# Gated attention on one NeuronCore: six gate tiles moved from VectorE quotients to ScalarE, and one order of products and idle matmuls for all passes

## What is computed

```python
scale = HEAD_DIM ** 0.5
scores = jnp.einsum('bhqd,bhkd->bhqk', q, k) / scale
scores = jax.nn.sigmoid(scores - mu) * jnp.exp(scores)
scores = scores / jnp.sum(scores, axis=-1, keepdims=True)
out = jnp.einsum('bhqk,bhkd->bhqd', scores, v)
```

## Time and profile before

| | us |
|---|---|
| median of three executions | 1508.39 |
| lowest, highest | 1506.9, 1511.1 |
| the profiled execution | 1511.61 |
| its span in the profile | 1509.7 |
| granted TensorE clock, mean | 0.948 of full |
| TensorE matmuls busy | 1274.5 (84%) |
| VectorE busy | 1133.8 (75%) |
| ScalarE busy | 1120.9 (74%) |
| POOL busy | 349.2 (23%) |

### The profile page before, as it was taken

The page is one execution under the profiler, slowest core; times in us unless marked ns, Lnnn a source line. Parts: engine busy times, 40 slices in busy tenths (PEclk is TensorE's granted clock), DMA queues, the critical chain, the costliest instruction groups (busy, mean ns, idle before and its releaser), DMA issues.

```text
span 1509.7 us, 22834 instructions
## 1 busy us (share of the span) xinstructions
PE 1274.5 (84%) x8290; PEld 657.9 (44%) x8290; DVE 1133.8 (75%) x2049; ACT 1120.9 (74%) x1604; POOL 349.2 (23%) x434
## 2 busy tenths in 40 slices
PE   6599999885888888888888887788999988888996
PEld 3244444462111111122111245566777866666774
DVE  8888886366697887976779656768756676776898
ACT  4177788747999999999999633455476576877985
POOL 2500001541000000002000034545555557431000
PEclk9599999996899999999999997999999999999998
DMA  5300100004000000100000120013333243011111
GB/s 191 111 24 25 44 24 4 2 5 150 0 22 18 4 22 1 37 21 1 21 1 0 57 92 1 1 31 96 94 112 91 78 112 140 21 36 29 43 50 56
DMA packets 41088, 70.50 MB, mean 47 GB/s; under 512 B 6416, under 2 KB 14864, under 8 KB 40208
## 3 DMA queue, kind: packets, MB, share of 16 engines
q1 hardware_dynamic: 40976, 69.05, 15.0%
HBM read 59.26 MB, written 9.76 MB: 46 GB/s over the span
## 4 chain that ended last, share of the span: by engine, by line
PE 32%; DVE 26%; ACT 20%; issue 13%; POOL 6%; DMA 2%; SPq 1%; POOLq 0%; ACTq 0%; DVEq 0%
ACT SHARED L1144 12%; DVE SHARED L1180 8%; PE PS L823 5%; PE PS L787 3%; PE PS L645 2%; DVE PS L2255 2%; PE PS L712 2%; PE PS L2045 2%; PE PS L2047 2%; PE PS L2046 2%; PE PS L1359 2%; DVE X L284 1%; POOL SHARED L2078 1%; PE PS L2054 1%; DVE STX L266 1%
## 5 line engine op out<-in xcount | busy, mean ns | idle before, releaser
L1144 ACT ACTIVATE SHARED<-PS 128x1536 f32<-128x1536 f32 (+1 forms) x346 | 457.5, 1449 | 14.8 <-PE PS L1036 9.8
L1180 DVE TENSOR_TENSOR SHARED<-SHARED 128x1536 f32<-128x1536 f32 (+1 forms) x170 | 276.6, 1700 | 34.7 <-ACT SHARED L1144 34.7
L1036 PE MATMUL PS<-QS,KS 48*128 48x512 bf16 (+1 forms) x1006 | 208.2, 397 | 83.0 <-ACT SHARED L1144 76.5
L803 ACT ACTIVATE SHARED<-PS 128x512 f32<-128x512 f32 (+3 forms) x384 | 163.6, 493 | 72.1 <-PE PS L791 63.6
L1036 PEld LDWEIGHTS PS<-QS,KS 48*128 48x128 bf16 (+1 forms) x1006 | 38.3, 94 | 297.8 <-ACT SHARED L1144 271.1
L2045 PE MATMUL PS<-ROUNDED 128*128 128x512 f32 x328 | 138.0, 421 | 15.7 <-DVE ROUNDED L2242 7.8
L1049 PE MATMUL PS<-SHARED,Vg 128*16 128x512 f32 x1024 | 139.5, 619 | 7.2 <-DVE SHARED L1180 6.9
L732 DVE TENSOR_REDUCE NM<-PS 128x2 f32<-128x1024 f32 (+3 forms) x128 | 124.0, 1018 | 13.2 <-PE PS L718 12.6
L2047 PE MATMUL PS<-ROUNDED 128*128 128x512 f32 x328 | 130.7, 398 | 0.0
L2046 PE MATMUL PS<-ROUNDED 128*128 128x512 f32 x328 | 130.5, 398 | 0.0
L2175 ACT ACTIVATE ROUNDED<-PS 128x512 fp32r<-128x512 f32 x100 | 59.8, 598 | 91.8 <-DVE PS L2255 91.8
(11 more groups left out here) (279 smaller groups left out, 2483.6 us busy)
## 6 DMA issues: line engine op xcount, KB each, us to landing
SHARED<-wx SPq DMA_DIRECT2D x64, 256.0 KB, 3.2
SHARED<-in_moe SPq DMA_DIRECT2D x3, 1600.0 KB, 10.8
SHARED<-wx SPq DMA_DIRECT2D x16, 224.0 KB, 2.9
SHARED<-kx SPq DMA_DIRECT2D x32, 96.0 KB
KS<-kx SPq DMA_DIRECT2D x32, 96.0 KB
SHARED<-wx SPq DMA_DIRECT2D x16, 192.0 KB, 2.8
SHARED<-wx SPq DMA_DIRECT2D x16, 160.0 KB, 2.8
qx<-SHARED SPq DMA_DIRECT2D x16, 128.0 KB, 2.4
```

Of the source, the lines that this page charges most:

```text
L803: act.activation(PB[t % 3][:, h, q0:CH], bank(RING0[n % 3], q0), ACT.Exp, scale=SCORE_SCALE)\
L1036: ins = pe.matmul(bank((v % 2) * GRP + f - a), KS[g % 2][r, h // 2, kt * P:kt * P + P], QS[g % 2][r, h // 2, qh * CH:(qh + 1) * CH], start ...
L1144: act.activation(dst, PS[:, (v % 2) * GRP * CH:((v % 2) * GRP + b - a) * CH], ACT.Exp if second == qh else ACT.Sigmoid, scale=SCORE_SCALE)\
L1180: dve.tensor_tensor(ex_tile(j), ex_tile(j), GR[w % RING][:, 0:(b - a) * CH], ALU.mult)\
```

## The change

`QUOTIENT`, `WEIGHT_LATE` and the two functions of the quotient are taken out. All 16 passes have 11 gate tiles, scored by TensorE (3 more matmuls in each of the six passes), activated by ScalarE (1 more tile in each) and multiplied by VectorE. All follow `WEIGHT_AT` and `FILL_AT`. ScalarE's activation for exp(mu) and its wait ahead of the stage are gone.

```diff
-        WEIGHT_LATE = (6, 7, 9, 11, 13, 15, 17, 19)
...
-        QUOTIENT = (0, 2, 4, 6, 8, 14)
-        QS1 = [arena(24064, CH), arena(31744, CH), arena(31744 + CH, CH)]
-        EMU = MU1[:, 3:4]
-
-        def by_quotient(n, j):
-
-            return n % 2 == 1 and n // 2 in QUOTIENT and j == 0
-
-        SCORED = [(n, j) for n in range(4 * NG) for j in range(NTILE) if not by_quotient(n, j)]
+        SCORED = [(n, j) for n in range(4 * NG) for j in range(NTILE)]
...
         def pe_tile(pe, n, j):
...
-            if by_quotient(n, j):
-                return
...
-                            if (WEIGHT_LATE if hf in QUOTIENT else WEIGHT_AT)[kt] == at:
+                            if WEIGHT_AT[kt] == at:
                                 pe_weighted1(pe, hf, kt)
...
-                            pe_keep_clock(pe, n // 4, FILL_AT.get(at, 2 if at == 5 and hf in QUOTIENT else 0))
+                            pe_keep_clock(pe, n // 4, FILL_AT.get(at, 0))
...
         def act_gated(act):
-            act.wait_ge(mu_rows, 1)
-            act.activation(EMU, col("mu"), ACT.Exp).then_inc(mu_rows, 1)
             for n in range(4 * NG):
...
                 for j in range(NTILE):
-                    if by_quotient(n, j):
-                        continue
...
-        def dve_quotient_begin(dve, own, hf):
-
-            dve.wait_ge(mu_rows, 2)
-            dve.wait_ge(A[1, "s_act"], NTH[2 * hf, 0] + 1)
-            for i in range(GRP):
-                ins = dve.tensor_scalar(QS1[i], EX[:, i * CH:i * CH + CH], EMU, 1e-37, ALU.add, ALU.max)
-            own.link(ins)
-            for i in range(GRP - 1):
-                own.mark(dve.reciprocal(QS1[i], QS1[i]))
-
-        def dve_quotient_end(dve, own, hf):
-            own.link(dve.reciprocal(QS1[GRP - 1], QS1[GRP - 1]))
-            for i in range(GRP):
-                ins = dve.tensor_tensor(QS1[i], EX[:, i * CH:i * CH + CH], QS1[i], ALU.mult)
-            own.link(ins)
-            for i in range(GRP):
-                e = EX[:, i * CH:i * CH + CH]
-                ins = dve.tensor_tensor(e, e, QS1[i], ALU.mult)
-            ins.then_inc(A[1, "mul"], 1)
...
         def dve_gated(dve, own):
-            dve.wait_ge(A[1, "part2"], 2 * NC)
-            dve_quotient_begin(dve, own, 0)
             for hf in range(QH * NG):
-                if hf in QUOTIENT:
-                    dve_quotient_end(dve, own, hf)
                 for j in range(NTILE):
-                    if by_quotient(2 * hf + 1, j):
-                        continue
...
                 dve_beside_gated(dve, own, hf + 1)
-                if hf + 1 in QUOTIENT:
-                    dve_quotient_begin(dve, own, hf + 1)
                 dve.wait_ge(A[1, "pv"], KT * (hf + 1))
```

## The result

Six executions of the changed kernel took 1498.97 to 1503.73 us, median 1502.59; six of the kernel before, now with three more beside the new ones, 1506.9 to 1511.57, median 1509.32. The ratio is 0.9949, 95% interval 0.9935 to 0.9963: the change saves about 7 us, 0.5%. The forecast was 1504.7 us in a range of 1501.0 to 1509.0. The time lies in the range. But the gain is almost twice the 3.7 us of the sum, and it is "faster by over 0.3%", which had been given 0.37, and not "same", which had been given 0.56.

What follows compares the result with a forecast made beforehand. ScalarE sets the stage's pace, with VectorE late because of the quotient. Terms 0.43 - 1.55 - 0.80 - 0.79 - 0.80 - 0.21 = -3.72 us take the median 1508.39 to 1504.7 us, range 1501.0 to 1509.0.

Steps and rivals of the forecast that it cites:

- 0.54 us wait for scores: ScalarE's one wait for scores in pass 4, put down to TensorE's 8 idle matmuls; expected to go.
- Passes 2, 4, 6, 14: Their table periods become like passes 1 and 12, 30.25 us: -1.55, -0.80, -0.79, -0.80 us.
- Pass 0: TensorE at low clock; 1.23 us wait stays, 0.92 becomes 0.15; period 31.20 to 31.63 us, +0.43.
- ScalarE's start: Without the small Exp, the first table load should still lie ahead of the wait for scores: 0; otherwise +1.28 us.
- loads: SyncE's loads in the stage, released by score tile counts that name the same tiles as before: 0.
- POOL: Its copies in the stage, released by weighted products that come no later: 0.
- Pass 8: Its period goes from 30.53 us to that of pass 9, 30.32 us: -0.21 us.
- clock falls: Drops of TensorE's granted clock in the stage stay as many as they were; forecast case, chance 0.65.
- rival A: TensorE's clock falls in the new passes, at the short last gate tile; all six falling gives 1514.2 us; chance 0.08.
- B: ScalarE's waits were not the quotient's, so six tiles are simply added: +8.1 us, 1516.4 us; chance 0.03.
- C: Nothing measurable: pass 0's low bound and one more clock fall against the rest, 1508.3 us; chance 0.10.
- D: More gained: clock also stays up in pass 7's period, or pass 0 loses nothing; 1503.2 us; chance 0.14.

Runs made afterwards that it cites:

- short reciprocals: Kernel before with each of the 18 VectorE reciprocals made over 32 of its 512 columns, quotients kept; ratio 0.9919, stage 478.68 us.
- single quotient: Kernel before with a quotient in pass 14 alone; ratio 0.9979, pass 14 at 31.05 us.
- order alone: Kernel before with quotients kept, but one order of products and idle matmuls for all passes; ratio 1.0015, stage 493.40 us.
- second profile: Kernel before run and profiled once more with no edit; ratio 1.0001, stage 492.40 us.
- two-block quotients: Kernel before with the short two-block tile first in each pass, two reciprocals per quotient, one order; six passes 0.9905, eight 0.9946, six with second reciprocal moved 0.9904.

## Why the prediction was right, and where it fell short

**The mechanism holds.** ScalarE's chain sets the stage, and the quotient gave back more than its tile because VectorE came late. The unbroken passes, the short reciprocals and the single quotient show it from three sides: 30.17 without, 31.05 with, 28.83 if VectorE is on time.

The prediction had one reading wrong, that of the 0.54 us wait for scores. It put that wait down to the 8 idle matmuls with one tile missing. With short reciprocals the idle matmuls are the same and the tile is missing too, and the wait is gone, so it came from VectorE's late copy. The forecast did not suffer, since the wait was expected to go with the quotient.

**Passes 2, 4, 6, 14.** The sum had -1.55, -0.80, -0.79, -0.80; the profile has -1.62, -0.88, -0.87, -0.88. I had taken 30.25, pass 1's length, where pass 12's 30.18 fits an even pass.

**Pass 0.** +0.43 forecast, +0.49 measured, with the one wait near 1.2 us. The two parts are shown apart: the order alone is -1.03 with the quotient kept, and -0.63 (32.35 to 31.72) with all tiles on ScalarE; the tile and its waits are the rest.

**ScalarE's start, loads, POOL.** Forecast 0, and the periods show nothing.

**Pass 8 was mis-sized.** -0.21 was the difference to a 30.53 that stood behind a clock fall. In the second profile the pass takes 31.26, so the term is about -0.93. The two rows stood side by side in the earlier trace rows, 31.84 and then 30.53, and I read each by itself. That the first pair of profiles shows -0.20 against the -0.21 of the sum is luck: it is the same short row that both start from.

**The clock falls were mis-sized, on the other side from rival A.** I forecast that they stay as many as they were, and gave the side on which they vanish 0.14. In the first pair of profiles this is nearly the whole miss: pass 7 gave -1.59 where the sum had 0, and -5.55 + 1.59 = -3.96 is left against -3.72. The kernel before had a fall in pass 2 in both of its profiles and one, then two, in passes without a quotient (7; 5 and 11). With a quotient list of six and the tiles cut as before, four profiles have 36 periods of passes without a quotient and 5 falls in them. The four profiles without quotients and the one with a quotient in pass 14 alone, up to pass 13, have 69 periods behind pass 0 and no fall. Each fall costs about 1.5 us when nothing catches up behind it (31.83 - 30.33 in pass 11). So with this cut of the tiles the falls go with the quotients. Why a quotient brings a fall in another pass is open, but the traces narrow it down. The place is the one that the prediction named for rival A: all five begin some 15 us behind the table load (14.9 to 15.1, from windows of 1 us), when TensorE comes to the tile behind the short last gate tile. These are its matmuls for the short tile and for the next one, in pass 7 of the kernel before and then of the changed kernel:

```profile
606.20 0.39 PE L1036 MATMUL PS<-QS,KS 48*128 48x512 bf16 x2
607.46 0.99 PE L1036 MATMUL PS<-QS,KS 48*128 48x512 bf16 x3 [0.87 <-ACT SHARED L1144]
...
601.51 0.39 PE L1025 MATMUL PS<-QS,KS 48*128 48x512 bf16 x2
602.77 0.59 PE L1025 MATMUL PS<-QS,KS 48*128 48x512 bf16 x3 [0.87 <-ACT SHARED L1129]
```

The wait of 0.87 us and the distance from the table load, 14.98 us, are the same, and only the first has the fall. The three kernels with two-block quotients, whose last gate tile is a whole one, have 25 periods of passes without a quotient and no fall in them, though their periods are uneven too (29.61 and 30.12). At 5 in 36 one would expect three or four. So neither quotients nor uneven periods seem to suffice by themselves. The short last gate tile may be needed as well, but no run has changed it alone.

Together: two profiles of the kernel before have stages of 490.89 and 492.40, and the three of kernels with no quotient and the new order 485.24 to 485.38. That is 5.5 to 7.2 us, against 3.7 in the sum. The ratios of the three sets, 0.9949, 0.9968 and 0.9967, make 4.8 to 7.7 us. So I take 1.25 + 1.8 of the 8.6 us between the first two spans as scatter of the size seen above, and the rest is the stage.

**The rivals.** A did not occur; the kernel without idle matmuls shows what it would have been. B falls with the result, which is below the kernel before and not 8.1 us above it, and with the short reciprocals. C is excluded by the intervals. D's first part is what happened, and not its second; but it is not the "matter of how the falls happen to lie in time" that I called it, since the other three profiles without quotients have no fall either.

## What to carry to other kernels

Work that moves from a full engine to one with idle time pays only if it ends before the first engine's next deadline. Look at how late the receiving engine's next instruction starts, not at its busy share: here a quotient made VectorE 12.9 us busier in two periods (26.65 + 24.55 against 2 x 19.16), left it far from full, and cost 0.88 us net, and one of two blocks with a reciprocal put into a wait was worth 0.91 us (29.20 against 30.11, pass 12 of the same kernel). When one period's row is to price an edit, read the row ahead of it too: a stall there may have paid a part already.

## What the runs showed of the hardware

- A fall of the granted clock to 0.50 for some 3 us costs 1.5 us in a pass where TensorE is otherwise 80% busy, but only about 0.8 in two passes together when the next one has a late VectorE to catch up (31.81 + 30.32 against 30.25 + 31.04).
- Here 18 idle matmuls of 0.2 us in each pass hold the clock at 1.00; without them it is at half rate for 10 of 31 us.
- A reciprocal of 128 x 512 takes 3.3 us on VectorE, twice the 1.63 us of a product of three times that size (17.91 / 11).
- The same instructions ahead of the stage (but for the small Exp, which some profiles lack) took 358.9 to 359.8 us at a mean granted clock of 0.93 and 366.4 us at 0.89, so this kernel of 1.5 ms moves by several us where nothing was edited.
